# The root of the squares' sums moves from GpSimd to VectorE, and the scaling by it to the next turn

## The reference

```python
def attn_layer(x, Wqkv, qs, ksc, Wo):
    q, k, v = split(x @ Wqkv)             # 16 heads of 64
    q = q / max(norm(q), 1e-12) * qs      # norm over a head's 64 elements
    k = k / max(norm(k), 1e-12) * ksc
    q = q * cos * scale + rotate_half(q) * sin * scale
    k = k * cos / scale + rotate_half(k) * sin / scale
    return local_attention(q, k, v) @ Wo  # windows of 32, each with the one before

for i in range(6):
    x = attn_layer(shift_tokens(x), Wqkv[i], q_scale[i], k_scale[i], Wo[i]) + x
    x = ffn_layer(shift_tokens(x), ln_g[i], ln_b[i], W1[i], b1[i], W2[i], b2[i]) + x
```

## Time and profile before

| | us |
|---|---|
| Median of 3 runs | 2357.19 (2354.05 to 2358.03) |
| The profiled execution | 2350.51 |
| Its span in the profile | 2348.3 |
| TensorE busy | 2016.3 (86%) |
| VectorE busy | 1561.5 (66%) |
| GpSimd busy | 1489.8 (63%) |
| ScalarE busy | 1308.2 (56%) |
| Mean granted clock of TensorE | 0.911 |

### The profile page before, as it was taken

One profiled execution on the slowest core, in us unless ns is written; L12 is line 12 of the kernel. 1 busy time (PEld: TensorE's weight loads), 2 busy tenths in 40 slices (PEclk: granted clock), 3 DMA queues, 4 the chain that ended last, 5 costly groups with the idle time before them and its releaser, 6 DMA issues. The chain is left out here.

```text
span 2348.3 us, 75381 instructions
## 1 busy us (share of the span) xinstructions
PE 2016.3 (86%) x33032; PEld 1379.1 (59%) x33032; DVE 1561.5 (66%) x1657; ACT 1308.2 (56%) x1547; POOL 1489.8 (63%) x2073
## 2 busy tenths in 40 slices
PE   3679898688998997989989889899899798998986
PEld 1234434366666665666666666666666566666664
DVE  5556552476776776767767767677776676776763
ACT  1145446455664665646656656566466464665652
POOL 1000000798886968878868788788686887885950
PEclk7589989798998999999989989999999899899997
DMA  2310100122222222322223322233222232222221
GB/s 87 112 48 30 52 23 11 44 69 64 58 78 62 64 64 69 86 59 58 62 54 80 87 54 66 53 78 80 63 62 64 68 85 61 58 58 55 63 62 41
DMA packets 132872, 146.33 MB, mean 62 GB/s; under 512 B 60856, under 2 KB 75452, under 8 KB 131776
## 3 DMA queue, kind: packets, MB, share of 16 engines
q1 hardware_dynamic: 132544, 141.51, 23.9%
HBM read 30.51 MB, written 5.44 MB: 15 GB/s over the span
## 5 line engine op out<-in xcount | busy, mean ns | idle before, releaser
L736 DVE TENSOR_TENSOR arena<-arena,rn 128x1024 f32<-128x1024 f32 x192 | 289.6, 1550 | 442.8 <-POOL rn L1085 442.8
L1109 POOL TENSOR_TENSOR arena<-arena,tab_sl 128x512 f32<-128x512 f32 x384 | 544.0, 1447 | 12.6 <-ACT arena L931 7.1
L1117 POOL TENSOR_TENSOR arena<-arena 128x1024 f32<-128x1024 f32 x192 | 470.4, 2472 | 0.0
L960 ACT ACTIVATE arena<-arena 128x1024 f32<-128x1024 f32 x96 | 101.5, 1058 | 554.6 <-DVE arena L767 554.6
L471 PE MATMUL banks<-w_qkv,arena 128*128 128x512 f32 x768 | 368.5, 624 | 12.0 <-DVE arena L799 6.4
L538 PE MATMUL banks<-arena 64*64 64x32 f32 x12288 | 254.7, 227 | 19.1 <-DVE arena L767 19.0
L548 PEld LDWEIGHTS banks<-w_o,arena 128*128 128x128 f32 x1536 | 204.5, 209 | 104.5 <-DVE X L810 65.5
L538 PEld LDWEIGHTS banks<-arena 64*64 64x64 f32 x12288 | 243.8, 140 | 33.5 <-DVE arena L767 22.2
L639 DVE TENSOR_REDUCE arena<-banks 128x1 f32<-128x1024 f32 (+7 forms) x176 | 175.1, 1027 | 126.1 <-PE banks L372 125.7
L548 PE MATMUL banks<-w_o,arena 128*128 128x128 f32 x1536 | 208.6, 294 | 57.2 <-DVE X L810 57.2
L471 PEld LDWEIGHTS banks<-w_qkv,arena 128*128 128x128 f32 x768 | 143.6, 197 | 169.1 <-issue 151.8
(11 more groups left out here) (112 smaller groups left out, 3215.8 us busy)
## 6 DMA issues: line engine op xcount, KB each, us to landing
arena<-arena SPq DMA_DIRECT2D x1512, 64.0 KB, 2.0
w_qkv<-Wqkv SPq DMA_DIRECT2D x6, 1024.0 KB, 5.4
arena<-parts_dram SPq DMA_DIRECT2D x96, 48.0 KB
arena<-parts_dram SPq DMA_DIRECT2D x32, 144.0 KB
parts_dram<-arena SPq DMA_DIRECT2D x4, 768.0 KB, 3.3
w_o<-Wo SPq DMA_DIRECT2D x6, 512.0 KB
w_qkv<-Wqkv SPq DMA_DIRECT2D x6, 512.0 KB, 4.2
arena<-X SPq DMA_DIRECT2D x24, 128.0 KB
```

The lines of the kernel that those rows point to most:

```text
L736: e.tensor_tensor(to, to, rn[n % 2][:, HEADS * m:HEADS * (m + 1)].unsqueeze(2).to_broadcast([P, HEADS, HEAD_DIM]), ALU.mult).then_inc(S["r ...
L1109: e.tensor_tensor(qk_sw[:, m, :].rearrange("p (h d) -> p h d", d=HEAD_DIM)[:, :, d:d + HALF], raw[:, m, :].rearrange("p (h d) -> p h d", d ...
L1117: e.tensor_tensor(to, to, qk_sw[:, m, :], ALU.add).then_inc(S["rs"], 1)
```

## The change

The root leaves GpSimd and goes to VectorE, directly behind the sum of squares of the same tile. It is now 11 instructions: the floor and the first guess as `scalar_tensor_tensor` with a second tensor operand (the sums themselves, and a tile `magic` that holds the constant), and three Newton steps of three instructions, a `tensor_tensor` and two `scalar_tensor_tensor`. `scale` moves from the end of the turn of tile n+1 to the beginning of the turn after it, ahead of the subtraction and behind line 810. GpSimd's turn keeps the memsets, the rotation and `ff_rsqrt`; the memsets wait for its own additions and for the sine table, where they had waited for rn.

```diff
--- before.py
+++ after.py
@@ -98,7 +98,7 @@
 parts0_out parts1_out xa_in rows_out ya_out ya_back out_done
 ln_step x_norm masks_b wdiag ones_set a_xT a_xnT a_proj a_hi a_rest a_mid a_lo a_vproj a_va va_set
 a_sc a_max a_mstep a_mlo a_mT a_mrows a_wsc a_exp a_gather a_acc a_accT a_recip a_cat a_out a_y
-tab_c tab_s halves_set zero_xs zero_xf row_in xsT xs_ready proj raw sq ss_sum newton rn rc sw rs rot tk tq kt_ready qt_ready kp
+tab_c tab_s halves_set magic_set zero_xs zero_xf row_in xsT xs_ready proj raw sq ss_sum newton rn rc sw rs rot tk tq kt_ready qt_ready kp
 sc mx sub v_proj v_ready vw_first ex sm recip p_norm pT pt pv ot wo x_attn
 f_stat f_mv f_var f_rstd xf_norm f_nT xft h gel u_one u f_out x_ff final""".split()
 
@@ -143,6 +143,7 @@
         base_c, base_s = sb("base_c", [P, tiles, 2, HEAD_DIM]), sb("base_s", [P, tiles, 2, HEAD_DIM])
         X = sb("X", [P, all_tiles, P])
         RS = 2 * HEADS
+        magic = sb("magic", [P, RS])
         rs_h, rs_t, rs_g, minus_half = sb("rs_h", [P, RS], I32), sb("rs_t", [P, RS]), sb("rs_g", [P, RS]), sb("minus_half", [P, GROUP])
         stats = sb("stats", [P, 6])
         mean_var = sb("mean_var", [P, all_tiles, 2])
@@ -605,7 +606,7 @@
 
         def vector_program(e):
             w = Once(e)
-            ln_step = Count()
+            ln_step, newton = Count(), Count()
 
             def ln_rsqrt(n, sem, count):
 
@@ -724,9 +725,26 @@
 
             def norms(n):
                 w.wait_ge(S["sq"], 2 * n + 2)
-                w.wait_ge(S["rn"], max(0, n - 1))
-                e.tensor_reduce(ss[n % 2][:, :], qk_sq.rearrange("p m (h d) -> p (m h) d", d=HEAD_DIM), AX_X, ALU.add
-                                ).then_inc(S["ss_sum"], 1)
+                y, v, t = rn[n % 2][:, :], ss[n % 2][:, :], rs_g[:, :]
+                w.wait_ge(S["rot"], max(0, 2 * (n - 1)))
+                e.tensor_reduce(v, qk_sq.rearrange("p m (h d) -> p (m h) d", d=HEAD_DIM), AX_X, ALU.add).then_inc(S["ss_sum"], 1)
+                w.wait_ge(S["ss_sum"], n + 1)
+                e.scalar_tensor_tensor(out=v, in0=v, scalar=NORM_FLOOR ** 2, in1=v, op0=ALU.max, op1=ALU.max
+                                       ).then_inc(S["newton"], newton.up())
+                w.wait_ge(S["newton"], newton.n)
+                w.wait_ge(S["magic_set"], 1)
+                e.scalar_tensor_tensor(out=y.bitcast(I32), in0=v.bitcast(I32), scalar=-0.5, in1=magic[:, :], op0=ALU.mult, op1=ALU.add
+                                       ).then_inc(S["newton"], newton.up())
+                for i in range(3):
+                    w.wait_ge(S["newton"], newton.n)
+                    e.tensor_tensor(t, y, y, ALU.mult).then_inc(S["newton"], newton.up())
+                    w.wait_ge(S["newton"], newton.n)
+                    e.scalar_tensor_tensor(out=t, in0=t, scalar=-0.5, in1=v, op0=ALU.mult, op1=ALU.mult).then_inc(S["newton"], newton.up())
+                    w.wait_ge(S["newton"], newton.n)
+                    last = e.scalar_tensor_tensor(out=y, in0=t, scalar=1.5, in1=y, op0=ALU.add, op1=ALU.mult)
+                    if i < 2:
+                        last.then_inc(S["newton"], newton.up())
+                last.then_inc(S["rn"], 1)
 
             def scale(n):
                 w.wait_ge(S["rn"], n + 1)
@@ -815,6 +833,8 @@
                 ff_here = s >= FF and G < n_groups
                 if s >= FF and k == 1 and G > 0:
                     ff_residual(G - 1)
+                if 0 <= s - 2 < n_tiles:
+                    scale(s - 2)
                 if 0 <= s - 3 < n_tiles:
                     subtract(s - 3)
                 if 0 <= s - 1 < n_tiles:
@@ -826,8 +846,6 @@
                 if 0 <= s - 3 < n_tiles:
                     sums(s - 3)
                     normalise(s - 3)
-                if 0 <= s - 1 < n_tiles:
-                    scale(s - 1)
                 if ff_here and k == 1:
                     ff_stats(G)
                 if ff_here and k == 3:
@@ -1024,8 +1042,8 @@
 
         def gpsimd_program(e):
             w = Once(e)
-            newton = Count()
             e.memset(minus_half[:, :], -0.5).then_inc(S["halves_set"], 1)
+            e.memset(magic[:, :], RSQRT_MAGIC).then_inc(S["magic_set"], 1)
             e.memset(VA, 0.0).then_inc(S["va_set"], 1)
             w.wait_ge(S["va_set"], 1)
             e.memset(VA[:, :, :, A_DIM:A_DIM + 1], 1.0).then_inc(S["va_set"], 1)
@@ -1065,28 +1083,6 @@
             w.wait_ge(S["zero_xf"], 1)
             e.memset(uT[64:P, nf - 1, :], 1.0).then_inc(S["u_one"], 1)
             w.wait_ge(S["u_one"], 1)
-
-            def norms(n):
-                y, v, t = rn[n % 2][:, :], ss[n % 2][:, :], rs_g[:, :]
-                w.wait_ge(S["ss_sum"], n + 1)
-                w.wait_ge(S["rot"], max(0, 2 * (n - 1)))
-                e.tensor_scalar(v, v, NORM_FLOOR ** 2, None, ALU.max).then_inc(S["newton"], newton.up())
-                w.wait_ge(S["newton"], newton.n)
-                e.tensor_scalar(y.bitcast(I32), v.bitcast(I32), -0.5, RSQRT_MAGIC, ALU.mult, ALU.add
-                                ).then_inc(S["newton"], newton.up())
-                for i in range(3):
-                    w.wait_ge(S["newton"], newton.n)
-                    e.tensor_tensor(t, y, y, ALU.mult).then_inc(S["newton"], newton.up())
-                    w.wait_ge(S["newton"], newton.n)
-                    e.tensor_tensor(t, t, v, ALU.mult).then_inc(S["newton"], newton.up())
-                    w.wait_ge(S["newton"], newton.n)
-                    e.tensor_scalar(t, t, -0.5, 1.5, ALU.mult, ALU.add).then_inc(S["newton"], newton.up())
-                    w.wait_ge(S["newton"], newton.n)
-                    last = e.tensor_tensor(y, y, t, ALU.mult)
-                    if i < 2:
-                        last.then_inc(S["newton"], newton.up())
-                last.then_inc(S["rn"], 1)
-                w.wait_ge(S["rn"], n + 1)
 
             def ff_rsqrt(G):
                 w.wait_ge(S["f_mv"], GROUP * (G + 1))
@@ -1118,7 +1114,8 @@
 
             def first_values(n):
                 w.wait_ge(S["pv"], max(0, n - 2))
-                w.wait_ge(S["rn"], n)
+                w.wait_ge(S["rs"], 2 * n)
+                w.wait_ge(S["tab_s"], 2 * (n // all_tiles + 1))
                 for hp in range(2):
                     e.memset(Vw[n % 3][64 * hp:64 * hp + WINDOW, 0, :], 0.0).then_inc(S["vw_first"], 1)
                 w.wait_ge(S["vw_first"], 2 * (n // tiles + 1))
@@ -1133,7 +1130,6 @@
                     rotate(s - 1)
                     if s < n_tiles and s % all_tiles == 0:
                         load_sin(s // all_tiles)
-                    norms(s - 1)
                 if s >= FF and k == 1 and G < n_groups:
                     ff_rsqrt(G)
```

## The result

| | before | after |
|---|---|---|
| Median of the runs, us | 2355.62 (4 runs) | 2739.63 (2737.03 to 2742.12, 4 runs) |
| Span of the profiled execution, us | 2348.3 | 2740.2 |
| Mean granted clock of TensorE | 0.911 | 0.852 |

The kernel became slower by the factor 1.163 (95% interval 1.161 to 1.165), 384 us. The forecast was 2830, its range 2600 to 2950.

The account below looks back on a forecast made before the run. It took waits between VectorE, GpSimd and TensorE, not TensorE's busy share, as the bound. Four turns of 98.55 us against 77.9 gave +459, early turns +26, last turns -11: 2350.5 becomes 2825, forecast 2830 us, range 2600 to 2950.

Parts of the forecast that it names:

- The root beside GpSimd: VectorE's root: each instruction meeting GpSimd's rotation waits out one whole GpSimd instruction; 2.5 us undisturbed, up to 11.6.
- The phase: GpSimd's sine products start 5.4 us into the turn, during the root's fourth instruction; the next four wait, three run free.
- The turns: Four turns walked at 23.1, 17.2, 29.0 and 26.8 us, 98.55 together with memsets and clock, against 77.9 before.
- Luck at k = 2: With GpSimd a rotation behind, six root instructions wait, the root ends at 13.65 and the turn takes 29.0 us.
- The memsets: GpSimd delayed every eighth tile: that turn 2.3 us shorter, the next 2.8 longer, 0.25 in four turns.
- six early turns: Turns without a feed-forward part at the start: 20.7 us each against 98.7 together before, +26 us.
- The upper bound: 2950 us, if the clock costs its 6 us in four turns (+85 us) and each root meets one more GpSimd addition.
- The clock: TensorE's granted clock falls in longer idle stretches: nothing to some 6 us in four turns, taken as 2.2.
- A: Rival: small VectorE instructions aren't held up by GpSimd, only large ones; 82.9 us in four turns, 2475 us; chance 0.11.
- B: Rival: faster, the root hides in VectorE's idle time and every four turns take 71.35 us; some 2210 us; chance 0.05.
- C: Rival: relief and cost cancel, time within 0.2% of 2357 us; chance 0.02.
- The wait for the root: VectorE's 362 us wait for GpSimd's root: the removal's most possible worth, but not by itself a gain.

Follow-up runs that it names:

- E1: Changed kernel with the root left out and eleven chained reductions of the same size, one SBUF operand each, in its place: 2440.17 us.
- E8: Changed kernel with one Newton step instead of three, so five root instructions instead of eleven: 2536.68 us.
- E2: Changed kernel with an added wait: GpSimd's rotation of a tile starts only after the previous tile's root is through: 2592.27 us.
- E9: Changed kernel with the root left out and eleven tensor_scalar products by 1.0, one SBUF operand each, in its place: 2760.06 us.
- E7: Changed kernel with GpSimd's two memsets one turn later: 2766.68 us.
- E4: Kernel before, with scale alone moved to the beginning of the next turn and the root left on GpSimd: 2385.02 us, ratio 1.014.
- E6: Kernel before, with the k = 1 statistics ahead of scale and the two memsets one turn later: 2227.08 us, ratio to before 0.947.
- E5: Kernel before, with the k = 1 statistics ahead of scale instead of behind it: 2334.13 us, ratio 0.993.

## Why the prediction was right, and where it was off

- **The root beside GpSimd.** Right, and it is the case. The extrapolation from 1024 elements to 32 held: the caught instructions take one GpSimd instruction each. E1, E8 and E2 show it, each in another way, and E9 shows that it isn't the exchange of the root for stand-ins that made E1 fast.
- **The phase.** Right: the sine products start 5.5 us into the turn, and four instructions run before them, four with them and three after, as walked.
- **The turns.** The walk without the clock's share has 23.1, 17.2, 29.0 and 26.8. Measured are 23.7, 16.6 and mostly 27.0 for k = 0, 1 and 3 where no memset stands near, and 29.9 as the mean of all k = 2 turns. The clock's 2.2 us were never shared out among the turns beforehand, so how near each comes with its part isn't a finding.
- **Luck at k = 2.** The walk let six instructions be caught and had the root end at 13.65. In most turns it is seven, and in the turn shown the root ends at 15.55 (1684.90 less 1669.35). TensorE's transposed weights (520 now) end 24.2 us into the turn there, not at 20.5, but from their end to the next maximum it is 6.8 us, not 8.5. The five short turns then bring the mean of 30.9, 29.7 and 27.3 down to 29.9. Errors of opposite sign made this turn fit.
- **The memsets** are the term with the wrong size: 0.25 us in four turns. I let GpSimd's delay by them start only in the turn after. They stand in the queue through the k = 3 turn as well, which is 22.7 instead of 27.0: 4.3 us in every eighth turn, some 48 us of the 90 by which the forecast was too high. The two turns behind were to be 2.3 shorter and 2.8 longer; they came out at 22.3 instead of 23.7 and at 17.9 instead of 16.6, which is another 7 us or so. E7 shows the cause. It moves the total by 27 us only, because the k = 0 and k = 1 turns get shorter by it, by 0.9 and 0.6 us on average.
- **Smaller terms.** The k = 1 turn was 0.6 us too long in the walk, some 14 us; six early turns came out at 119.3 instead of 124.2. The rest, some 15 us, lies in the mean of the other turns and wasn't traced further.
- **The upper bound.** The 85 us for the clock end at 2915. One more addition 1117 in each root would be 2.4 us in every turn, over 200 us, and not the 35 that are left up to 2950. So the upper end doesn't follow from the sum that it names; nothing measured came near it.
- **The clock.** Its direction was right: the mean granted clock fell to 0.852, and the transposes of k and q, which come right behind TensorE's idle time, took 385 ns each on average, 299 before (the page's group of line 480). I priced that at 2.2 us in four turns. The group took 95 us more busy time than before (311.8 against 216.8), some 4 us in four turns, and how much of it lay on the path no run isolates. The price is open.
- **Rivals.** A is refuted as a mechanism: small instructions are held up, and the root's are all of the plain two-operand form. E1 shows that its walk, 2475, was good to 35 us. B is refuted: without the port the change still costs 84 us. The rule of the Trainium skill that stood beside B (Perfetto Trace Analysis, section Optimizing GPSIMD Operations), to prefer other engines to GpSimd, would have led astray here. C is out by the result.
- **The wait for the root.** The prediction said that its 362 us were no gain by themselves. E4 shows how little: 205 us less of it, and the kernel 29 us slower.

## What to carry to other kernels

Before small dependent work moves from GpSimd to VectorE, look at what GpSimd will be doing at that moment: each small instruction of a form that GpSimd's work holds up can cost a whole instruction of GpSimd's, so count how many fall into its busy time, and where the work allows it pick a form that doesn't wait (here the reduction). In a profile this shows as busy time, not as waiting: compare the mean of a small instruction with its smallest. And of two waits on an engine, the one that stands in the queue a turn too early can matter more than the longer one: moving two memsets gave 107 us in the kernel before (E6 against E5), where more than halving the other wait alone gave nothing (E4). But the worth of such a move belongs to its kernel: in the changed kernel the same one cost 27 us (E7).

## What was not expected of the hardware

- A `tensor_scalar` of 32 elements with a single SBUF operand waits for GpSimd just as a two-operand instruction does (463 ns on average in its largest group, E9), and a reduction of the same size doesn't (186 ns, E1).
- Beside a memset of GpSimd's, which only writes, the two-operand forms run free (0.19 us, with E7) and the `tensor_scalar` waits (0.53 and 0.54 us, with E9). This was so in all ten turns of either trace in which the two meet.
- The hold works both ways, and GpSimd's instruction can be small too. Its line 1090, 4 elements, took 1.05 us on average, as it meets the product of `scale` (0.225 us before, when it was line 1094). The group, and one meeting of the two:

```profile
L1090 POOL TENSOR_SCALAR ln_v<-mean_var 128x4 f32<-128x4 f32 x24 | 25.3, 1053 | 390.2 <-DVE mean_var L809 390.2
```

```profile
1287.83 2.34 DVE L754 TENSOR_TENSOR arena<-arena,rn 128x1024 f32<-128x1024 f32 x2
...
1288.01 1.13 POOL L1090 TENSOR_SCALAR ln_v<-mean_var 128x4 f32<-128x4 f32 x1 [19.58 <-DVE mean_var L809]
```
